# Linear attention in groups of four chunks, with weights laid out as TensorE reads them

## The chip, the cores and the metric

The program runs on one core of one Trainium2 chip. Its metric is device time in microseconds (us), the median of several runs; lower is better. All tensors that matter here are float32.

## The reference

The program is a hybrid network of eight layers over 2048 tokens of 512 features (`x = x + layer(layernorm(x))`): a complex recurrence, a feed-forward layer, a state space scan, the same feed-forward layer, softmax attention, a mixture of experts, a linear attention and the mixture of experts again. Only the seventh, the linear attention, is touched. It has H = 32 heads of D = 64:

```python
qkv = silu(hidden_states @ qkv_w.T).reshape(b, s, H, 3 * D)   # qkv_w: (6144, 512)
q, k, v = split(qkv, 3, axis=-1)                               # then cut into blocks of tokens
def step(state, blk):
    qi, ki, vi = blk
    aw = einsum('bhid,bhjd->bhij', qi, ki) * dd                # scores inside the block, with decay
    intra = einsum('bhij,bhjd->bhid', aw, vi)
    inter = einsum('bhid,bhde->bhie', qi * qd_, state)
    new_state = state * bd_ + einsum('bhsd,bhse->bhde', ki * kd_, vi)
    return new_state, intra + inter
attn = rmsnorm(attn over all 2048 head features, norm_w)
gate = sigmoid(hidden_states @ gate_w.T)                       # gate_w: (2048, 512)
return gate * attn @ out_w.T                                   # out_w: (512, 2048)
```

x has the shape (1, 2048, 512), so that here b = 1 and s = 2048, and the state runs over all 2048 tokens.

## The kernel before

Each layer is a block of its own: every engine has its own program, written out by hand in order, and semaphores are waited on by count. There is a barrier between blocks. The kernel works with its own block length of CH = 128 tokens (a chunk; NCH = 16 chunks), which gives the same values as any other block length. NB = 512 tokens are a quarter (TQ = 4 chunks; TC = 4 quarters). Two heads form a pair: 128 features on the 128 partitions; PAIRS_L = 16 pairs.

The layer has three blocks. `lina` normalizes the residual and transposes it to `lin_z`, features by tokens. `linb` (`linear_heads`) makes the heads. `linc` (`linear_outputs`) multiplies by the output weights.

`linear_heads` holds, for each pair, four kinds of projections (KINDS = 4: query, key, value, gate), each of 128 features by 2048 tokens. A piece (`piece`, L2165) is one kind for one quarter: four matmuls (one for each 128 of the 512 input features) with a 128 x 128 slice of weights `wt` held still and 512 tokens of `z` streaming, into one of two PSUM buffers `pr_ps`; ScalarE takes it out through Silu or Sigmoid (`piece_out`, L2259). The trace shows every float32 matmul as two records and a transpose as one. The weights arrive as rows of features (`wr`), so that before the first piece of a kind TensorE transposes four 128 x 128 blocks (`weight`, L2157, with its records under L2162) and ScalarE copies them to `wt` (`weight_out`, L2255). These five uses of `pr_ps` in each kind make the 20 USES of a pair.

While pair n is scanned, the pieces of pair n + 1 are projected: between the two halves of each chunk stands one piece. `body` (L2227) runs for every chunk c:

- `chunk_first` (L2177): scores of both heads (`s_ps`, L2185, 64 rows each, two heads in the two halves of the array), a transpose of the keys (L2188) and one of the values (L2189) to `tr_ps`. ScalarE brings them out as `kt`, times a decay (two instructions, L2271), and `vt` (L2273). VectorE makes `aw` = scores times decay (L2363).
- the piece of the next pair, and after each fourth the weights of the next kind.
- `chunk_second` (L2191): values times `aw` into `o_ps` (L2201, 64 columns each), the state of the chunks before times `qd` into the same (L2207), then the addition of this chunk to the state, `kv_ps` (L2212). VectorE updates the state, one instruction for each head (L2347).

After each fourth chunk ScalarE copies `o_ps` to `osb` (L2279), POOL adds its squares to `squares` (L2147, L2149), VectorE makes `gated` (L2369) and SyncE stores it. At the start of a pair VectorE makes `qd`, all 2048 tokens in one instruction (L2357), ahead of the first `aw`. Before the first pair, POOL fills tables (L2127 to L2140) for which TensorE and ScalarE wait, ScalarE makes decays (L2287), and the 16 pieces of pair 0 are projected with nothing beside them. In the last pair there is no next one, and so no piece.

`linear_outputs` sums the squares on TensorE (L2420), loads `out_w` in four parts of 1 MB and the first gated features in two of 2 MB, transposes 64 blocks of weights (L2429, L2448), waits for all of them (until 4890.4 in the trace), and then does 16 tiles of 128 tokens, 16 matmuls each (L2438).

Of the kernel before, what the change touches and what calls it, by code (L numbers as in the profile page):

```python
# [21 lines left out]
P = 128  # L22
T = 2048
D = 512
# [1998 lines left out]
def linear_heads(nc, g, name, z, squares):  # L2023
# [3 lines left out]
    with Layer(nc, name) as L:  # L2027
        TQ = NB // CH
        USES = KINDS * (TC + 1)
        wr = L.sb("wr", [P, KINDS, D])  # L2030
        wt = L.sb("wt", [P, KINDS, DT, P])
        proj = [L.sb(f"proj{b}", [P, KINDS, T]) for b in range(2)]
        qd = L.sb("qd", [P, T])
# [10 lines left out]
        aw = L.sb("aw", [P, 2, CH])  # L2044
        kt = L.sb("kt", [P, 2, LD])
        vt = L.sb("vt", [P, P])
        state = L.sb("state", [P, 2, P])
# [4 lines left out]
        s_ps = L.ps("s_ps", [P, 2, 4, CH])  # L2052
        tr_ps = L.ps("tr_ps", [P, 4, P])
        kv_ps = L.ps("kv_ps", [P, 4, P])
        o_ps = L.ps("o_ps", [P, 2, NB])
        names = ("w_taken", "pr_done", "pr_out", "consts", "tables0", "tables", "qd_done", "s_done", "aw_done", "tr_done",
                 "vt_done", "kv_done", "state_done", "o_done", "o_out", "gated_done", "sq_step", "sq_done",
                 "norm_loaded", "osb_used", "state_step", "act_passed")
        S = {n: L.sem(n) for n in names}
        (w_taken, pr_done, pr_out, consts, tables0, tables, qd_done, s_done, aw_done, tr_done, vt_done, kv_done,  # L2060
         state_done, o_done, o_out, gated_done, sq_step, sq_done, norm_loaded, osb_used, state_step, act_passed) = (S[n] for n in names)
        w_loaded = [L.sem(f"w_loaded{k}") for k in range(KINDS)]
        saved = [L.sem(f"saved{b}") for b in range(2)]
        block = L.block()
        qkv_rows = g.dram["L1_attn_b_qkv_w"].rearrange("(h c r) i -> h c r i", c=3, r=LD)
        gate_rows = g.dram["L1_attn_b_gate_w"].rearrange("(n p) i -> n p i", p=P)
# [3 lines left out]
        def over_pairs(eng, body):  # L2070

            with eng.Fori(0, PAIRS_L // 2 - 1) as r:
                body(r * 2, 0, False)
                body(r * 2 + 1, 1, False)
            body(PAIRS_L - 2, 0, False)
            body(PAIRS_L - 1, 1, True)

        @block.sync
        def _(sp):
            def load(kind, n):  # L2080
                if kind < 3:
                    for hh in range(2):
                        sp.dma_start(wr[hh * LD:(hh + 1) * LD, kind:kind + 1, :],
                                     qkv_rows[bass.ds(n * 2 + hh, 1), kind, :, :].rearrange("h r i -> r h i")).then_inc(w_loaded[kind], 16)
                else:
                    sp.dma_start(wr[:, kind:kind + 1, :], gate_rows[bass.ds(n, 1), :, :].rearrange("n p i -> p n i")).then_inc(w_loaded[kind], 32)

            def save(n, b, q):
# [5 lines left out]
            def reload(kind, n):  # L2094

                if kind == 0:
                    sp.wait_ge(pr_done, (n - 1) * USES + 1)
                else:
                    sp.wait_ge(pr_done, (n - 1) * USES + (5 * (kind - 1) + 6))
                sp.sem_inc(w_taken, 1)  # L2100
                load(kind, n)
# [3 lines left out]
            for kind in range(KINDS):  # L2105
                load(kind, 0)
            for kind in range(KINDS):
                reload(kind, 1)


            with sp.Fori(0, PAIRS_L // 2 - 1) as r:
                for b in range(2):
                    n = r * 2 + b
                    for q in range(TC):
                        reload(q, n + 2)
                        save(n, b, q)
            for b in range(2):
                for q in range(TC):
                    save(PAIRS_L - 2 + b, b, q)
            for b in range(2):  # L2120
                sp.wait_ge(saved[b], 16 * (PAIRS_L * TC // 2 + 1))
            sp.wait_ge(norm_loaded, 16)

        @block.gpsimd
        def _(pool):
# [17 lines left out]
            def body(n, b, last):  # L2143
# [12 lines left out]
        def _(pe):  # L2156
            def weight(kind, n, use):  # L2157

                pe.wait_ge(w_loaded[kind], n * 32 + 32)
                pe.wait_ge(pr_out, use[0] * USES + (use[1] + 1))  # L2160
                for k in range(DT):
                    last = nc.tensor.transpose(pr_ps[:, use[1] % 2, k * P:(k + 1) * P], wr[:, kind, k * P:(k + 1) * P], g.ident[:, :])  # L2162
                last.then_inc(pr_done, 1)

            def piece(kind, t, n):  # L2165

                use = 5 * kind + t + 1
                pe.wait_ge(pr_out, n * USES + (5 * kind + 2))
                pe.wait_ge(pr_out, n * USES + (use + 1))
                if t == 0:  # L2170
                    pe.wait_ge(pr_out, n * USES + (5 * kind + 3))
                for k in range(DT):
                    last = nc.tensor.matmul(pr_ps[:, use % 2, :], wt[:, kind, k, :], z[:, k, t * NB:(t + 1) * NB],  # L2173
                                            start=(k == 0), stop=(k == DT - 1))
                last.then_inc(pr_done, 1)

            def chunk_first(n, b, c):  # L2177
                m = n * NCH + c
                cols = slice(c * CH, (c + 1) * CH)
                if c == 0:  # L2180
                    pe.wait_ge(pr_out, n * USES + (USES + 2))
                pe.wait_ge(aw_done, m + 1)
                for hh in range(2):
                    rows = slice(hh * LD, (hh + 1) * LD)
# [342 lines left out]
```

## Time and profile before

| | us |
|---|---|
| median of 3 runs (lowest, highest) | 5951.64 (5946.49, 5953.91) |
| the profiled execution | 5950.2 |
| its span | 5948.2 |
| `linb`, from its first instruction to the barrier behind it | 3374.1 to 4860.3 |
| `linc`, to the last output matmul | 4860.3 to 5110.4 |

The profile is of one execution. The times of rows are counted from the start of the span. PE is TensorE's matmuls, PEld its weight loads, DVE VectorE, ACT ScalarE, POOL GpSimd, SP SyncE. PEclk is the clock that TensorE was granted, as a share of 2.4 GHz; 0.50 is 1.2 GHz. A matmul's duration is longer than the step from one to the next, since they are pipelined: the steps are read from start times.

### The profile page before, as it was taken

How to read it: one execution, taken by the hardware profiler on the slowest of the kernel's cores; microseconds unless marked ns; L12 is line 12 of the kernel's file. 1: busy time of each engine (PE TensorE's matmuls, PEld its weight loads, DVE VectorE, ACT ScalarE, POOL GpSimd, SP SyncE). 2: the span in 40 equal slices, each digit the busy share in tenths (PEclk: the TensorE clock that was granted, in tenths of full speed). 3: DMA queues.
4: the chain of work that ended last, by engine and by line, in shares of the span. 5: the costliest groups of instructions: out<-in, count | busy, mean ns of one | idle time of the engine just before them, and what ended most of it. 6: DMA issues, size and time to landing. Idle time of an engine off the chain costs nothing. (4 is left out here: it accounts for less than half of the span.)

```text
span 5948.2 us, 67863 instructions
## 1 busy us (share of the span) xinstructions
PE 5051.6 (85%) x25328; PEld 2536.2 (43%) x25328; DVE 2334.4 (39%) x3377; ACT 1822.7 (31%) x3499; POOL 1525.2 (26%) x951
## 2 busy tenths in 40 slices
PE   6037897799999999859999499999999979689997
PEld 3013343333333332356555245445445444455654
DVE  1853678357666667441221212222222220331111
ACT  2412554211555457421111133333333320121111
POOL 0011000102776772114545201111111110034444
PEclk9568999899999999969999799999999969789998
DMA  1000000000000000037888300000000012348887
GB/s 44 0 18 12 11 0 0 30 0 1 1 1 1 1 1 1 34 125 204 219 220 225 67 20 25 25 21 25 25 23 23 20 68 71 135 128 224 221 225 161
DMA packets 227748, 395.20 MB, mean 66 GB/s; under 512 B 31712, under 2 KB 119776, under 8 KB 226912
## 3 DMA queue, kind: packets, MB, share of 16 engines
q1 hardware_dynamic: 170144, 249.14, 12.6%
q0 software_dynamic: 57344, 142.64, 11.8%
q8 instruction: 158, 2.59, 0.2%
q14 instruction: 102, 0.84, 0.0%
HBM read 288.88 MB, written 107.02 MB: 67 GB/s over the span
## 5 line engine op out<-in xcount | busy, mean ns | idle before, releaser
L2173 PE MATMUL linb_pr_ps<-lin_z,linb_wt 128*128 128x512 f32 x2048 | 944.5, 606 | 9.0 <-ACT linb_wt L2257 9.0
L1365 ACT ACTIVATE attc_prob<-attc_ps 128x512 f32<-128x512 f32 x1024 | 548.9, 597 | 443.2 <-PE attc_ps L1276 442.4
L1239 POOL TENSOR_TENSOR attc_acc<-attc_acc,attc_prob 128x2048 f32<-128x2048 f32 x120 | 547.9, 4566 | 121.6 <-ACT attc_prob L1365 109.3
L1389 DVE TENSOR_REDUCE attc_peak<-attc_ps 128x2 f32<-128x1024 f32 x384 | 469.6, 1225 | 257.9 <-PE attc_ps L1284 257.9
L2173 PEld LDWEIGHTS linb_pr_ps<-lin_z,linb_wt 128*128 128x128 f32 x2048 | 380.6, 196 | 398.6 <-issue 388.7
L1276 PE MATMUL attc_ps<-att_q,att_k 32*128 32x512 f32 x2048 | 528.7, 616 | 0.0
L2347 DVE SCALAR_TENSOR_TENSOR linb_state<-linb_state,linb_sdec,linb_kv_ps 64x64 f32<-64x64 f32 x448 | 125.3, 280 | 859.0 <-PE linb_kv_ps L2212 851.8
L1284 PE MATMUL attc_ps<-att_k,att_q 32*128 32x512 f32 x1536 | 449.9, 663 | 0.0
L2147 POOL TENSOR_TENSOR linb_sq<-linb_osb 128x512 f32<-128x512 f32 x64 | 67.5, 1055 | 1295.1 <-ACT linb_osb L2279 1295.1
L2262 ACT ACTIVATE linb_proj<-linb_pr_ps 128x512 f32<-128x512 f32 x256 | 152.8, 597 | 625.5 <-PE linb_pr_ps L2173 625.4
L1297 PE MATMUL attc_ps<-attc_prob,att_v 128*32 128x256 f32 (+1 forms) x3472 | 316.5, 437 | 0.3 <-ACT attc_prob L1365 0.3
L886 DVE TENSOR_TENSOR_SCAN ssmb_state<-ssmb_decay,ssmb_bu 128x2048 f32<-128x2048 f32 x64 | 279.7, 4409 | 78.9 <-ACT ssmb_decay L833 78.9
L1864 POOL DMA_INDIRECT residual_rows<-moe2c_ye,moe2w_index x128 | 202.1, 1579 | 313.2 <-issue 279.8
L1864 POOL DMA_INDIRECT residual_rows<-moe1c_ye,moe1w_index x128 | 202.0, 1578 | 311.7 <-issue 279.5
L770 PE MATMUL ssmb_y_ps<-ssmb_state,ssmb_diag 128*128 128x512 f32 x512 | 241.2, 618 | 39.9 <-DVE ssmb_state L886 30.0
L1273 PE MATMUL attc_ps<-att_rows,attc_ones 32*128 32x512 bf16 x1024 | 240.8, 391 | 11.0 <-ACT attc_prob L1365 9.4
L1897 PE MATMUL moe2c_gu_ps<-moe2c_xt,moe2w_wgu 128*128 128x256 f32 x1024 | 249.4, 400 | 0.0
L1897 PE MATMUL moe1c_gu_ps<-moe1c_xt,moe1w_wgu 128*128 128x256 f32 x1024 | 245.6, 396 | 0.0
L215 PE MATMUL lrud_y_ps<-lrud_w,lrud_ht 128*128 128x512 f32 x128 | 56.7, 606 | 216.4 <-DMA lrud_bias<-in_L_attn_a_b_out 216.4
L2271 ACT ACTIVATE linb_kt<-linb_tr_ps,linb_kdec 128x64 f32<-128x64 f32 x512 | 133.0, 309 | 322.2 <-PE linb_tr_ps L2189 298.6
L2438 PE MATMUL linc_y_ps<-linc_wt,linc_gt 128*128 128x512 f32 x512 | 220.0, 592 | 1.0 <-ACT linc_wt L2448 1.0
L1897 PEld LDWEIGHTS moe2c_gu_ps<-moe2c_xt,moe2w_wgu 128*128 128x128 f32 x1024 | 203.0, 203 | 28.5
(516 smaller groups left out, 7766.7 us busy)
## 6 DMA issues: line engine op xcount, KB each, us to landing
moe1w_wgu<-in_L_ffn_gate_up_proj SPq DMA_DIRECT2D x32, 1536.0 KB, 12.4
moe2w_wgu<-in_L_ffn_gate_up_proj SPq DMA_DIRECT2D x32, 1536.0 KB, 12.4
moe1w_wd<-in_L_ffn_down_proj SPq DMA_DIRECT2D x32, 512.0 KB, 13.6
gated_features<-linb_gated SPq DMA_DIRECT2D x64, 256.0 KB, 2.1
linc_gt<-gated_features SPq DMA_DIRECT2D x8, 2048.0 KB, 8.3
moe2w_wd<-in_L_ffn_down_proj SPq DMA_DIRECT2D x32, 512.0 KB, 13.3
linb_wr<-in_L_attn_b_qkv_w SPq DMA_DIRECT2D x96, 128.0 KB, 2.6
residual_rows<-residual SPq DMA_DIRECT2D x2, 4096.0 KB, 12.9
```

The lines of the kernel that those rows point to most:

```text
L770: last = nc.tensor.matmul(y_ps[:, t, :], diag[:, s % DIAGS, :], state[:, s % RING, t * NB:(t + 1) * NB], start=(n == 0), stop=(n == N_STAT ...
L886: V.tensor_tensor_scan(state[:, s % RING, :], decay[:, s % RING, :], bu[:, e % 2, :], 0.0, ALU.mult, ALU.add).then_inc(state_done, 1)
L1239: pool.tensor_tensor(acc[:, n % 2, :, :], before, prob[:, U % NP, :, :], ALU.add).then_inc(pool_done, 2 if at == 1 else 1)
L1273: nc.tensor.matmul(ps[:, banks[-1], :], ones16[own, :], rows[own, cols], start=True, stop=False)
L1276: nc.tensor.matmul(ps[:, bank, :], k[own, f, keys], q[own, f, cols], start=False, stop=True).then_inc(s_done, 1)
L1284: last = nc.tensor.matmul(ps[:, bank + h % 2, :], q[own, f, i * P:(i + 1) * P], k[own, f, b * NB:(b + 1) * NB], start=True, stop=True)
L1297: last = nc.tensor.matmul(o_bank[h * DH:(h + 1) * DH, cols], v[:, i, at:at + DH], prob[:, U % NP, h, cols], start=(i == 0), stop=(i == TT ...
L1365: nc.scalar.activation(prob[:, U % NP, h, :], ps[:, n % 3 if at < 0 else at % 6, :], ACT.Exp).then_inc(exp_done, 1)
L1389: V.tensor_reduce(peak[:, w // TT % 2, i % QH, 2 * hp:2 * hp + 2, b], ps[:, bank:bank + 2, :], axis=AX.X, op=ALU.max).then_inc(mx_used, 1)
L1864: pool.indirect_dma_start(out=g.y_dram, out_offset=bass.IndirectOffsetOnAxis(ap=index[:, n // 2, n % 2:n % 2 + 1], axis=0), in_=ye[:, y % ...
L1897: last = nc.tensor.matmul(gu_ps[:, x, part, :], wgu[:, j % PW, x, k, part * IN:part * IN + P], xt[:, j % 2, x, k, :], start=(k == 0), stop ...
L2173: last = nc.tensor.matmul(pr_ps[:, use % 2, :], wt[:, kind, k, :], z[:, k, t * NB:(t + 1) * NB], start=(k == 0), stop=(k == DT - 1))
```

## The change

Nothing outside the layer changes. The parts:

1. The host lays three weights out (`LAYOUT`): qkv_w and gate_w so that the four 128 x 128 slices of each kind stand as TensorE takes them, out_w transposed. `weight`, `weight_out` and `wr` are gone. Each pair's weights come in two transfers (768 KB and 256 KB) into one of two buffers, two pairs ahead.
2. Values are projected token-major: for kind 2 the slices of `z` (128 tokens) are held still and 128 columns of weights stream, 16 matmuls in a piece in place of 4. ScalarE's Silu writes them straight to `vt[b]`; the transpose and the copy of the values are gone.
3. The scan goes by quarters of four chunks. On TensorE: all scores of the quarter, four key transposes (`keys_first`), one piece, the additions of four chunks (`additions`), three pieces, then all outputs of the quarter (`outputs`). ScalarE brings `kt` out with two instructions for four chunks (`keys_out`), VectorE makes `qd` for 512 tokens and `aw` for four chunks (128 x 1024) in one instruction each, and updates the state four times into 8 slots (`SLOTS`), with a wait between one update and the next.
4. `linear_outputs` loads `wt` directly, in four parts, alternating with four parts of the first features; the first tile waits for each part as it comes to it. The 64 transposes and 16 copies are gone.

```diff
-            def weight(kind, n, use):
-                pe.wait_ge(w_loaded[kind], n * 32 + 32)
...
+            def piece(kind, t, n, r, b):
+                use = TC * kind + t
+                if use == 0:
+                    pe.wait_ge(w_loaded[b], r * 32 + 32)
+                pe.wait_ge(pr_out, n * PIECES + (use + 1))
+                if kind == 2:
+                    for c in range(TQ):
+                        for k in range(DT):
+                            last = nc.tensor.matmul(pr_ps[:, use % 2, c * CH:(c + 1) * CH], z[:, k, (t * TQ + c) * CH:(t * TQ + c + 1) * CH],
+                                                    wt[:, b, kind, k, :], start=(k == 0), stop=(k == DT - 1))
+                else:
+                    for k in range(DT):
+                        last = nc.tensor.matmul(pr_ps[:, use % 2, :], wt[:, b, kind, k, :], z[:, k, t * NB:(t + 1) * NB],
+                                                start=(k == 0), stop=(k == DT - 1))
                 last.then_inc(pr_done, 1)
+            def keys_first(n, b, q):
+                m = n * TC + q
+                if q == 0:
+                    pe.wait_ge(pr_out, n * PIECES + (PIECES + 2))
                 pe.wait_ge(aw_done, m + 1)
+                for r in range(TQ):
+                    cols = slice(q * NB + r * CH, q * NB + (r + 1) * CH)
+                    for hh in range(2):
+                        rows = slice(hh * LD, (hh + 1) * LD)
+                        last = nc.tensor.matmul(s_ps[:, hh, r * CH:(r + 1) * CH], proj[b][rows, 1, cols], proj[b][rows, 0, cols],
+                                                start=True, stop=True)
                 last.then_inc(s_done, 1)
+                pe.wait_ge(kt_done, m + 1)
+                for r in range(TQ):
+                    cols = slice(q * NB + r * CH, q * NB + (r + 1) * CH)
+                    last = nc.tensor.transpose(tr_ps[:, r, :], proj[b][:, 1, cols], g.ident[:, :])
+                last.then_inc(tr_done, 1)
+            def additions(n, b, q):
+                m = n * TC + q
+                pe.wait_ge(kt_done, m + 2)
+                pe.wait_ge(state_done, m + 1)
+                for r in range(TQ - 1 if q == TC - 1 else TQ):
+                    last = nc.tensor.matmul(kv_ps[:, r, :], kt[:, r, :], vt[b][:, q * TQ + r, :], start=True, stop=True)
+                last.then_inc(kv_done, 1)
+            def outputs(n, b, q):
...
+            def body(n, r, b, more):
+                for q in range(TC):
+                    keys_first(n, b, q)
+                    if more:
+                        piece(q, 0, n + 1, r + b, 1 - b)
+                    additions(n, b, q)
+                    if more:
+                        for t in range(1, TC):
+                            piece(q, t, n + 1, r + b, 1 - b)
+                    outputs(n, b, q)
...
 # ScalarE, for each quarter: keys_out, the four piece_out, the table at q == 2, quarter_out
 # VectorE, for each quarter:
+                    V.tensor_tensor(qd[...], proj[b][:, 0, cols], qdec[...]).then_inc(qd_done, 1)
                     dve.wait_ge(s_done, m + 1)
+                    V.tensor_tensor(aw[...], s_ps[...], dd[...]).then_inc(aw_done, 1)
+                    update(n, q)
+                    dve.wait_ge(o_out, m + 3)
...
 # linear_outputs, SyncE
+            for j in range(4):
+                fs = slice(j * WF, (j + 1) * WF)
+                sp.dma_start(gt[:, 0, fs, :], g_rows[:, fs, 0:TOK]).then_inc(first[j], 16)
+                sp.dma_start(wt[:, fs, :], w_rows[:, fs, :]).then_inc(w_loaded[j], 16)
+            sp.dma_start(gt[:, 1, :, :], g_rows[:, :, TOK:2 * TOK]).then_inc(loaded[1], 16)
```

## Rows read from the trace of the kernel before

**Rows 1.** The page: busy time, share of the span and instructions of TensorE

```profile
PE 5051.6 (85%) x25328; PEld 2536.2 (43%) x25328; DVE 2334.4 (39%) x3377; ACT 1822.7 (31%) x3499; POOL 1525.2 (26%) x951
```

**Rows 2.** Windows: stretch, length, busy time and records by engine, clock, DMA share, GB/s

```profile
3633.00:3721.80 88.80, 86.94 (x367) 44.45 (x366) 22.78 (x51) 30.67 (x79) 10.54 (x8) 0.98 0.07 24
4786.20:4856.30 70.10, 49.83 (x221) 31.58 (x220) 21.74 (x51) 13.70 (x53) 12.62 (x8) 0.53 0.04 15
4860.30:4890.40 30.10, 20.14 (x96) 17.40 (x97) 0.23 (x2) 9.53 (x17) 0.00 (x0) 0.57 0.80 279
3728.70:3735.60 6.90, 6.90 (x23) 3.37 (x22) 0.87 (x3) 1.27 (x4) 0.00 (x0) 0.75 0.00 0
2528.00:2567.00 39.00, 39.00 (x182) 37.44 (x181) 8.82 (x27) 8.78 (x15) 0.00 (x0) 0.50 0.44 157
```

**Rows 3.** Timeline, TensorE, two chunks within a pair: start, us from there, line, records

```profile
3756.01 0.44 PE L2201 MATMUL linb_o_ps<-linb_aw,linb_vt 128*64 128x128 f32 x4
3756.38 0.49 PE L2207 MATMUL linb_o_ps<-linb_qd,linb_state 128*128 128x128 f32 x2
...
3757.03 0.49 PE L2185 MATMUL linb_s_ps<-linb_proj 64*128 64x128 f32 x4
3757.45 0.33 PE L2188 MATMUL linb_tr_ps<-ident,linb_proj 128*128 128x128 f32 x1
...
3757.73 3.60 PE L2173 MATMUL linb_pr_ps<-lin_z,linb_wt 128*128 128x512 f32 x8
3761.26 0.44 PE L2201 MATMUL linb_o_ps<-linb_aw,linb_vt 128*64 128x128 f32 x4
...
3766.93 0.44 PE L2201 MATMUL linb_o_ps<-linb_aw,linb_vt 128*64 128x128 f32 x4
```

**Rows 4.** Timeline, all engines, the first chunk of a pair

```profile
3724.61 2.93 DVE L2357 TENSOR_TENSOR linb_qd<-linb_proj,linb_qdec 128x2048 f32<-128x2048 f32 x1 [0.35 <-DVE linb_gated L2369]
...
3727.93 0.44 PE L2201 MATMUL linb_o_ps<-linb_aw,linb_vt 128*64 128x128 f32 x4 [1.86 <-DVE linb_aw L2363]
...
3729.57 5.13 PE L2173 MATMUL linb_pr_ps<-lin_z,linb_wt 128*128 128x512 f32 x8
```

**Rows 5.** Timeline, trains of small matmuls in the mixture of experts

```profile
2625.07 0.53 PEld L1790 LDWEIGHTS moe1b_lane_ps<-moe1b_split,moe1b_lane 128*128 128x128 f32 x4
...
2527.91 3.68 PE L1560 MATMUL moe1a_lg_ps<-moe1a_rwt,moe1a_zt 128*128 128x64 f32 x16
...
2800.69 2.60 PE L1907 MATMUL moe1c_gu_ps<-moe1c_xt,moe1w_wgu 128*64 128x256 f32 x22
```

**Rows 6.** The page: groups of VectorE and ScalarE, with busy us, mean ns

```profile
L1389 DVE TENSOR_REDUCE attc_peak<-attc_ps 128x2 f32<-128x1024 f32 x384 | 469.6, 1225 | 257.9 <-PE attc_ps L1284 257.9
L2347 DVE SCALAR_TENSOR_TENSOR linb_state<-linb_state,linb_sdec,linb_kv_ps 64x64 f32<-64x64 f32 x448 | 125.3, 280 | 859.0 <-PE linb_kv_ps L2212 851.8
L2271 ACT ACTIVATE linb_kt<-linb_tr_ps,linb_kdec 128x64 f32<-128x64 f32 x512 | 133.0, 309 | 322.2 <-PE linb_tr_ps L2189 298.6
```

**Rows 7.** Timeline, TensorE, two chunks of the last pair

```profile
4845.93 0.70 PE L2201 MATMUL linb_o_ps<-linb_aw,linb_vt 128*64 128x128 f32 x4 [0.96 <-ACT linb_vt L2273]
...
4850.09 0.70 PE L2201 MATMUL linb_o_ps<-linb_aw,linb_vt 128*64 128x128 f32 x4 [0.96 <-ACT linb_vt L2273]
```

**Rows 8.** Timeline, TensorE, the projections of pair 0

```profile
3388.40 1.11 PE L2162 MATMUL linb_pr_ps<-ident,linb_wr 128*128 128x128 f32 x4 [15.75 <-POOL linb_slope_own L2140]
3396.01 16.73 PE L2173 MATMUL linb_pr_ps<-lin_z,linb_wt 128*128 128x512 f32 x32 [6.50 <-ACT linb_wt L2257]
3412.57 0.60 PE L2162 MATMUL linb_pr_ps<-ident,linb_wr 128*128 128x128 f32 x4
3413.99 13.97 PE L2173 MATMUL linb_pr_ps<-lin_z,linb_wt 128*128 128x512 f32 x32 [0.82 <-ACT linb_wt L2257]
```

**Rows 9.** Transfers, two of four issued together: KB each, us from issue to landing

```profile
att_v<-in_L_attn_a_Wk SPq DMA_DIRECT2D x1, 1024.0 KB, 7.6
att_v<-in_L_attn_a_Wv SPq DMA_DIRECT2D x1, 1024.0 KB, 9.8
```

More of the change, by code:

```diff
@@ L2177, in chunk_first @@
[L2177 to L2181, printed above, removed]
-                pe.wait_ge(aw_done, m + 1)
-                for hh in range(2):
-                    rows = slice(hh * LD, (hh + 1) * LD)
-                    last = nc.tensor.matmul(s_ps[:, hh, 0, :], proj[b][rows, 1, cols], proj[b][rows, 0, cols], start=True, stop=True)
-                last.then_inc(s_done, 1)
-                pe.wait_ge(vt_done, m + 1)
-                nc.tensor.transpose(tr_ps[:, 0, :], proj[b][:, 1, cols], g.ident[:, :])
-                nc.tensor.transpose(tr_ps[:, 1, :], proj[b][:, 2, cols], g.ident[:, :]).then_inc(tr_done, 1)
@@ new lines, in additions @@
+            def additions(n, b, q):
[6 more added lines that the diff above has]
+            def outputs(n, b, q):
+                m = n * TC + q
+                out = o_ps[:, q % 2, :]
+                pe.wait_ge(o_out, m + 1)
+                pe.wait_ge(aw_done, m + 2)
+                for r in range(TQ):
+                    for hh in range(2):
+                        rows = slice(hh * LD, (hh + 1) * LD)
+                        last = nc.tensor.matmul(out[rows, r * CH:(r + 1) * CH], vt[b][:, q * TQ + r, rows], aw[:, hh, r * CH:(r + 1) * CH],
+                                                start=(r == 0), stop=(q == 0 and r == 0), skip_group_check=True)
+                pe.wait_ge(qd_done, m + 1)
+                pe.wait_ge(state_done, m + 2)
+                for r in range(TQ):
+                    c = q * TQ + r
+                    if c >= 1:
+                        last = nc.tensor.matmul(out[:, r * CH:(r + 1) * CH], state[:, c % SLOTS, :], qd[:, r * CH:(r + 1) * CH],
+                                                start=False, stop=True, skip_group_check=True)
+                last.then_inc(o_done, 1)
@@ L2247, in _ @@
+            over_pairs(pe, body)
         @block.scalar
@@ L2288, in _ @@
             table(0, 0)
-            weight_out(0, (0, 0))
             for kind in range(KINDS):
@@ L2412, in _, with tile @@
             for b in range(2):
-                sp.wait_ge(w_loaded[b], 32)
-                sp.wait_ge(loaded[b], 16 * (T // TOK // 2))
+                sp.wait_ge(loaded[b], 16 * (T // TOK // 2 - 1 + b))
         @block.tensor
         def _(pe):
+            def tile(b, s, used, fresh):
+                pe.wait_ge(y_used, used)
+                for f in range(FT):
+                    if fresh and f % WF == 0:
+                        pe.wait_ge(first[f // WF], 16)
+                        pe.wait_ge(w_loaded[f // WF], 16)
+                    last = nc.tensor.matmul(y_ps[:, s, :], gt[:, b, f, s * P:(s + 1) * P], wt[:, f, :],
+                                            start=(f == 0), stop=(f == FT - 1))
+                last.then_inc(y_done, 1)
             pe.wait_ge(ones_ready, 1)
```

337 lines of the change are left out of this document (122 added, 215 removed).

## The prediction

> **What bounds the kernel now.** I read the page first: TensorE is busy 85% of the span, the others 39% or less [rows 1]. The change touches only the linear attention, so I asked for windows by stretch next. One pair of heads takes 88.8 us, of which TensorE is busy 86.9 at a clock of 0.98; VectorE is busy 22.8, ScalarE 30.7, POOL 10.5 (first row of [rows 2]). Fifteen pairs go like this, one after the other. The last pair, which has no projections beside it, takes 70.1 us at a clock of 0.53: a chain of waits (second row of [rows 2]). Then 30.1 us pass before the first output matmul, with the DMA engines at 0.80 and 279 GB/s (third row of [rows 2]). So three quarters of what follows is a question of TensorE's own time, and I went to its timeline.
>
> A chunk is a period of 5.25 us (3756.01 to 3761.26) with no idle time [rows 3]. By start times: outputs 0.37 (L2201), state and additions together 0.65 (L2207 to L2185), scores 0.42, transposes 0.28, and the piece 3.53. In the piece eight records of 512 columns take 3.60 us, the last one about 0.59, so the step is (3.60 - 0.59) / 7 = 0.43 us for 512 columns, and 0.107 for 128. Now count the small work by that step: outputs and scores are two side-by-side pairs of records each, state, additions and transposes six records, in all ten steps, 1.1 us; the piece is 3.44. That is 4.52 us, and the period is 5.25: 0.73 us are in none of the streams. They lie where the shape in the array changes (128 x 128 to 64-column halves, back, to 64-row halves, to transposes): four changes in a chunk, 0.18 us each. The trace shows nothing else there. Beside it, each fourth chunk takes 5.67 us (3761.26 to 3766.93), 0.42 more, for the weight transposes.
>
> At a pair's start there is one real stall. VectorE makes qd for 2048 tokens (2.93 us) before the first aw; TensorE idles 1.86 us for it, and behind it the clock falls, in the next chunk: eight records last 5.13 us in place of 3.60 [rows 4], at a granted 0.75 (fourth row of [rows 2]). Two long chunks, 3.4 us for a pair: 88.7 = 16 x 5.25 + 4 x 0.42 + 3.4 - 0.4 (the last addition, which is left out, and roundings).
>
> **The change part by part.** *The scan and the pieces.* The same records remain, less four value transposes in a quarter and four weight transposes. A pair after the change, in steps of TensorE:
> - three kinds of pieces, 96 records of 512 columns by 0.43: 41.3;
> - value pieces, 128 records of 128 columns. Now each has a weight load of 128 columns beside only 128 streaming. The nearest row: four loads in 0.53 us, the last 0.19, a step of 0.113 [rows 5] (L1790). At the low clock, 16 records with only 64 columns streaming take 3.68, the last about 0.42, a step of 0.217, in which only the load can be the limit; at the full clock that is 0.109 [rows 5] (L1560). I take 0.112: 14.3 (against 13.8 before);
> - scores 32 and outputs 32 side-by-side pairs by 0.107: 6.8. That such pairs stay side by side in a long train is shown by 22 records of 256 columns in 2.60 us, where one after the other they would need 4.7 [rows 5] (L1907);
> - key transposes 16, additions 30, state 30, by 0.112: 8.5;
> - shape changes, four in a quarter and no longer in a chunk: 16 x 0.18 = 2.9.
>
> Sum 73.8, against 88.7: 14.9 less. 48 shape changes give 8.6 of it, the stall 3.4, the weight transposes 1.7, the value transposes 1.8, and the value pieces take 0.5 back. The first of the fifteen pairs has no stall now, so 15 x 14.9 - 3.4 = 220 us. Ends: if tiled trains load their weights between the steps, a side-by-side pair costs 0.21 and not 0.107, 6.8 a pair or 102 less gain; if shape changes cost nothing when no wait stands beside them, 40 more.
>
> *What hides the rest.* In front of the additions PE waits for kt. Its cover is scores, transposes and one piece: 1.1 + 0.6 + 3.4 = 5 us. On ScalarE are queued ahead of it the copy of the outputs (0.6), then two kt instructions of 256 elements, which I put at 0.45 each (309 ns at 64 elements [rows 6]); with latencies 3.3 us, and 4.8 where the table of the next pair stands ahead. Hidden, by 0.2 us at the least. In front of the outputs PE waits for aw and the state. VectorE has the gating (1.6), qd of 512 (2.93 / 4 = 0.7), aw of 1024 (1.2 by the reduction of the same shape from PSUM [rows 6] (L1389)), four updates of two (0.28 each [rows 6] (L2347), with waits 2.8 in all), 6.3 us; the cover from the additions on is three pieces, 10.3. So qd, which now stalls a pair, is hidden; late next is kt, at no price as long as ScalarE is not 2 us later. Weights come two pairs ahead, 80 us for transfers of 1 MB; SyncE's saves queued behind a reload don't wait, since the pieces that it waits for were done a quarter before.
>
> *The last pair.* Without pieces the quarter is a chain at the low clock (step 0.213, shape change 0.35): scores 2.1, transposes 1.25, kt 1.2, additions 2.1, updates 3.0, state into outputs 2.3: 12 us, 48 for four, less 1 for what is left out at both ends, against 70.1, in which a chunk is 4.16 [rows 7]. 22 us less (by 10 to 28, as kt and the updates are slower or the clock recovers).
>
> *The start.* TensorE has its weights at 3388.4 and needs not wait 6.50 us for ScalarE's first copy: 3396.01 - 3388.40 = 7.6. Each later kind starts 3413.99 - 3412.57 = 1.4 earlier, and one set of transposes goes at the end (0.9) [rows 8]. Less the value pieces' 0.5: 12 us. ScalarE's decays still stand before its first Silu, but two PSUM buffers cover them.
>
> *The output stage.* Before the first tile now stand 1.5 MB and not 8. All four parts are 6 MB: at 279 GB/s (third row of [rows 2]) the last lands at 4860.8 + 22.5 + 2 = 4885; at 1 MB in 2.2 us, the difference of two transfers in flight [rows 9], 12 us earlier. The tile itself is 32 x 0.43 = 13.8 and starts after the sums (7 us), cold. So it ends between 4884 and 4888, where now it ends at 4890.4 + 13.8 = 4904. I take 19 (16 to 21). Fifteen tiles behind it are as before, each fed ahead.
>
> Sum: 220 + 22 + 12 + 19 = 273. From the profiled execution, 5950.2, it gives 5677; that lies 1.4 us under the median, so 5679 as a median.
>
> The Trainium skill speaks against part 2 of the change ("TensorE: Matmul & The Clock Gate", Back-to-back issue gap): for pairs of weight load and matmul at 128 columns it gives about 81 ns, where the matmul alone has 56. By that ratio, 1.45, the value pieces would be an estimated 0.155 us a record. The trace here disagrees with it in the L1790 row, 0.113.
>
> **The rivals.** *A, the loads show.* Behind a load that changes with each record, part of the load is not covered. For it: state and additions, four such records, take 0.65 us, 0.16 each [rows 3]. Against: 0.18 of that 0.65 is a shape change, and L1790. Price: 0.05 x 2048 records = 100 us, 5779. It is what the skill's ratio would do.
>
> *B, the excess belongs to the records, not to the changes of shape*: the 0.73 us in a chunk stay when chunks are grouped. Price 15 x 8.6 = 129 us: 5808. Against: the L1907 and L1790 trains.
>
> *C, the clock falls in the value pieces.* For it: under 39 us of 64-column records and transposes, TensorE busy all along, the granted clock was 0.50 (fifth row of [rows 2]). Against: those stream for half of each step; here the step is full, as in the chunk at 0.98. Price: 64 pieces of 32 x 0.213 = 6.8 in place of 3.6: 205 us, 5884.
>
> *D, slower: a wait for kt in each quarter.* ScalarE does osb, the table, and kt in order, and if their latencies add up to more than the one piece in front of the additions covers, TensorE idles in all 60 quarters and the clock falls after each, as at a pair's start now. One such fall costs 1.7 us behind 1.86 of idling [rows 4]. The gain is 273 / 60 = 4.6 us a quarter, so from a wait of 2.9 us on the kernel is slower; ScalarE's chain would need 8 us and not 3.3 to 4.8. At 3.5 us of waiting, 5.2 x 60 = 312: 5991. For it: the wait is new, and three pieces that could cover it stand behind it.
>
> **How the numbers follow.** The forecast 0.78 (own range 5645 to 5740: better shape changes on one side, half of the tiled loads on the other), A 0.07, B 0.05, C 0.05, D 0.05. The predicted time is 5679. The range 5640 to 5785 takes in the forecast and A, and leaves out B, C and D, with a little of the forecast. What this kernel's times can tell from no change is about 0.2%, 12 us. Faster by more than that are the forecast, A, B and C: 0.94; within it, C or D near its break-even: 0.01; slower 0.05.
>
> **What would show it.** A pair of 74 us, clock near 1.00; 32 records of a value piece within 3.6 us; no idle time of PE before L2201's successor at the pair's start; a last pair of 48 us; the first output tile done 24 to 28 us after the block starts; and VectorE's qd at 0.7 us. PE idle before the additions, with kt as its releaser, would speak for D; a granted clock under 0.8 in the third quarter of each pair for C; a step of 0.15 or more in the value pieces for A; quarters of 20 us and more with no idle time for B. If the moving of the chunks makes a stage after it later (both end with the same barrier, so I see none), the sum is wrong too.

## The result, and the profile after

| | before | after |
|---|---|---|
| median of 4 runs each (lowest, highest), us | 5952.77 (5946.49, 5955.22) | 5676.69 (5664.62, 5686.34) |
| the profiled execution, us | 5950.2 | 5669.14 |
| its span, us | 5948.2 | 5667.4 |

The ratio is 0.9537, 95% interval 0.9513 to 0.956. The forecast was 5679, with a range of 5640 to 5785.

I split both spans at the same points, by start times of TensorE's instructions:

| stretch | before | after | gain | forecast |
|---|---|---|---|---|
| end of `lina`'s transposes to the first scores | 86.8 | 75.3 | 11.5 | 12 |
| first scores of pair 0 to those of pair 15 | 1327.0 | 1123.2 | 203.8 | 220 |
| the last pair, to the start of `linc` | 74.3 | 35.3 | 39.0 | 22 |
| `linc`, to its last output matmul | 249.3 | 229.0 | 20.3 | 19 |
| everything else | | | 6.2 | 0 |
| sum (the difference of the spans) | | | 280.8 | 273 |

The sum is right to 3%, but two of its terms are off by 16 and 17 us in opposite directions. "Everything else" is code that no kernel here touches; in the eleven traces of this document it takes between 4196.9 and 4220.0 us, so that the 6.2 says nothing of the change. TensorE has more records than before and is busy for less time (against [rows 1]); the instruction queue fetched more (158 packets, 2.59 MB before). From the page of the kernel after:

```profile
PE 4820.4 (85%) x26288; PEld 2581.4 (46%) x26288; DVE 2362.7 (42%) x3233; ACT 1644.4 (29%) x2764; POOL 1527.4 (27%) x951
...
q8 instruction: 214, 3.51, 0.3%
```

TensorE's timeline, one quarter in which values are projected. It answers to [rows 3]; L2204 are outputs, L2211 state, L2177 scores, L2183 key transposes, L2159 value pieces, L2192 additions:

```profile
3705.11 1.09 PE L2204 MATMUL linb_o_ps<-linb_aw,linb_vt 128*64 128x128 f32 x16
3706.13 1.16 PE L2211 MATMUL linb_o_ps<-linb_qd,linb_state 128*128 128x128 f32 x8
3707.22 1.16 PE L2177 MATMUL linb_s_ps<-linb_proj 64*128 64x128 f32 x16
3708.31 0.66 PE L2183 MATMUL linb_tr_ps<-ident,linb_proj 128*128 128x128 f32 x4
3708.80 3.74 PE L2159 MATMUL linb_pr_ps<-linb_wt,lin_z 128*128 128x128 f32 x32
3712.38 1.06 PE L2192 MATMUL linb_kv_ps<-linb_vt,linb_kt 128*128 128x128 f32 x8
3713.27 10.88 PE L2159 MATMUL linb_pr_ps<-linb_wt,lin_z 128*128 128x128 f32 x96
3724.08 1.09 PE L2204 MATMUL linb_o_ps<-linb_aw,linb_vt 128*64 128x128 f32 x16
```

No row has an idle time. The first 32 value records take 3712.38 - 3708.80 = 3.58 us, 0.112 each, as I had chosen. The 96 behind them take 10.81, 0.06 more than 96 x 0.112, with the beginning of a shape change at their end. Two rows of the page for VectorE (busy us, mean ns):

```profile
L2331 DVE TENSOR_TENSOR linb_qd<-linb_proj,linb_qdec 128x512 f32<-128x512 f32 x64 | 90.3, 1412 | 90.4 <-ACT linb_proj L2249 75.8 <-DVE linb_gated L2339 12.7
L2334 DVE TENSOR_TENSOR linb_aw<-linb_s_ps,linb_dd 128x1024 f32<-128x1024 f32 x64 | 78.3, 1224 | 2.6 <-PE linb_s_ps L2177 0.5
```

The pairs after are not all alike. By the starts of their first scores they take 73.8, 75.9, 75.4, 76.3, 73.8, 76.2, 73.8, 75.7, 73.8, 76.0, 75.4, 75.7, 73.8, 73.8, 73.8 us. Seven are as forecast and eight are longer by 1.6 to 2.5; this is where the 16 us went. Windows of the first pair (pair 0), of the first 4.8 us of pair 2 and of its rest, then of the last pair and of the first output tile (columns as in [rows 2]):

```profile
3445.40:3519.70 74.30, 74.24 (x436) 48.68 (x438) 22.97 (x41) 19.74 (x34) 7.90 (x6) 1.00 0.07 26
3595.20:3600.00 4.80, 4.80 (x24) 3.32 (x25) 2.35 (x3) 1.85 (x3) 1.32 (x1) 0.64 0.58 198
3600.00:3671.00 71.00, 71.00 (x411) 46.39 (x411) 21.07 (x39) 17.83 (x32) 7.91 (x6) 1.00 0.05 17
4568.60:4599.10 30.50, 19.92 (x206) 16.38 (x204) 20.91 (x42) 5.71 (x13) 12.58 (x8) 1.00 0.09 35
4603.80:4624.70 20.90, 20.66 (x58) 12.88 (x59) 0.48 (x3) 1.46 (x2) 0.00 (x0) 0.70 0.99 343
```

What ends TensorE's idle time is read from its waits. Over the scan, and then the start of pair 2 in the timeline:

```profile
PE linb_s_ps L2177 <- issue: 12.7, 6, 2.4
```

```profile
3595.19 1.66 PE L2177 MATMUL linb_s_ps<-linb_proj 64*128 64x128 f32 x16 [2.08 <-issue]
```

"issue" is time in which the engine waited for nothing that the profile shows: no semaphore and no data. The six places are the starts of pairs 2, 4, ... 12, where TensorE's loop over two pairs (L2073) begins again. Behind two of them, in pairs 2 and 10, the granted clock falls as well, for 1.6 us more each. The trace has the branch itself, on TensorE's sequencer (count, shortest, median and longest ns). In the kernel before (L2240) its median was 208.

```profile
L2073 PEldq COMPARE_BRANCH  x7: 76/3600/3949, 3591.3 to 4493.1; - x7
```

TensorE's loop has 1784 instructions in the trace now and had 1597. One of the page's two instruction queues (q8, 16 KB a packet) goes with this loop: in the six passes behind long jumps (3592 to 4493) it moves 54 packets, nine a pass. In the kernel before it moves none in the six repeated passes (3630 to 4690).

```profile
q8 instruction: 54, 0.88, 0.4%
```

### The profile page after: what moved, and what is told of

Same layout as the page of the kernel before. It is cut to its first block and busy times, and to the rows that moved or that the text cites. A ratio compares the mean times of both kernels' runs of the same rounds, so it can differ in the third digit from the quotient of the medians.

```text
span 5667.4 us, 66951 instructions
## 1 busy us (share of the span) xinstructions
PE 4820.4 (85%) x26288; PEld 2581.4 (46%) x26288; DVE 2362.7 (42%) x3233; ACT 1644.4 (29%) x2764; POOL 1527.4 (27%) x951
## 5 line engine op out<-in xcount | busy, mean ns | idle before, releaser
L2163 PE MATMUL linb_pr_ps<-lin_z,linb_wt 128*128 128x512 f32 x1536 | 677.8, 595 | 16.4 <-POOL linb_slope_own L2133 16.4
L2163 PEld LDWEIGHTS linb_pr_ps<-lin_z,linb_wt 128*128 128x128 f32 x1536 | 286.1, 191 | 342.1 <-issue 324.8
L2339 DVE SCALAR_TENSOR_TENSOR linb_gated<-linb_osb,linb_norm_w,linb_proj 128x512 f32<-128x512 f32 x64 | 94.4, 1474 | 668.1 <-ACT linb_osb L2266 668.1
L2140 POOL TENSOR_TENSOR linb_sq<-linb_osb 128x512 f32<-128x512 f32 x64 | 70.1, 1095 | 1039.0 <-ACT linb_osb L2266 1039.0
L2249 ACT ACTIVATE linb_proj<-linb_pr_ps 128x512 f32<-128x512 f32 x192 | 114.7, 597 | 517.2 <-PE linb_pr_ps L2163 517.2
L2159 PE MATMUL linb_pr_ps<-linb_wt,lin_z 128*128 128x128 f32 x2048 | 233.8, 275 | 0.0
L2159 PEld LDWEIGHTS linb_pr_ps<-linb_wt,lin_z 128*128 128x128 f32 x2048 | 231.2, 192 | 0.5 <-issue 0.5
L1297 PEld LDWEIGHTS attc_ps<-attc_prob,att_v 128*32 128x32 f32 x3472 | 69.0, 109 | 340.2 <-ACT attc_prob L1365 173.0
```

The costliest lines, as they stand in the source:

```text
L1297: last = nc.tensor.matmul(o_bank[h * DH:(h + 1) * DH, cols], v[:, i, at:at + DH], prob[:, U % NP, h, cols], start=(i == 0), stop=(i == TT ...
L2159: last = nc.tensor.matmul(pr_ps[:, use % 2, c * CH:(c + 1) * CH], z[:, k, (t * TQ + c) * CH:(t * TQ + c + 1) * CH], wt[:, b, kind, k, :], ...
L2163: last = nc.tensor.matmul(pr_ps[:, use % 2, :], wt[:, b, kind, k, :], z[:, k, t * NB:(t + 1) * NB], start=(k == 0), stop=(k == DT - 1))
```

## The experiments

Theory: the loop's body has become too long for what TensorE's sequencer keeps, so the jump back waits for instructions to be fetched again. Rivals: the new order, the dense issue of the value pieces, or the weight transfers at a pair's start. Further experiments take the forecast's terms one by one. Unless said otherwise a kernel is derived from the one after. Medians of the kernel before in the two timed groups: 5947.31 and 5949.73.

**The loop written out.**

```diff
-            over_pairs(pe, body)
+            for n in range(PAIRS_L):
+                body(n, n // 2, n % 2, n < PAIRS_L - 1)
```

> The changed kernel with TensorE's loop over pairs written out (16 bodies, no branch back); the other engines keep their loops. In the changed kernel's trace the branch at the end of TensorE's loop body takes 3.3 to 3.9 us (0.2 us in the kernel before), TensorE then idles 1.9 to 2.5 us at six pairs' starts, and twice the clock falls behind it (1.6 us each): 16 us in all. Theory: the body has become too long for what holds TensorE's instructions, so that the jump back has to fetch them, and straight code is fetched ahead. Then every pair takes 73.8 us, no idle time of 2 us at a pair's start, and the time is 16 us less (5653 beside 5669). Rival: the idle time is a wait for another engine that stands at the same place (VectorE's or ScalarE's own loop ends there too): then it stays, and the time stays within 3 us. A third way: straight code is fetched late as well, and small gaps appear all over: slower than the changed kernel.

Measured: 5649.76 (5645.8 to 5655.59), ratio 0.9512 (0.9495 to 0.9528), 0.0025 or 15 us under that of the kernel after (the medians are 27 apart, from different groups of runs, and the two intervals overlap, so that the proof is in the trace). Every one of the fifteen pairs takes 73.8 us; the scan takes 1106.9, which is 16.3 less. The transfers and the order of work are untouched, and the start of a pair has no idle time:

```profile
3587.37 1.16 PE L2211 MATMUL linb_o_ps<-linb_qd,linb_state 128*128 128x128 f32 x8
3588.46 1.16 PE L2177 MATMUL linb_s_ps<-linb_proj 64*128 64x128 f32 x16
```

**A short loop.** Three of four matmuls of the value projection are left out, so that the values are wrong.

```diff
-                        for k in range(DT):
-                            last = nc.tensor.matmul(pr_ps[...], z[:, k, ...], wt[:, b, kind, k, :], start=(k == 0), stop=(k == DT - 1))
+                        last = nc.tensor.matmul(pr_ps[...], z[:, c, ...], wt[:, b, kind, c, :], start=True, stop=True)
```

> The changed kernel with three quarters of the value projections left out (each 128 x 128 block of values is made from 128 of the 512 input features, so the values differ from the reference's): TensorE's loop is kept, but its body is shorter by 384 instructions, shorter than that of the kernel before. It asks whether the length of the body makes the slow branch. Theory of the length: branches of about 0.2 us as in the kernel before, no idle time at pairs' starts, no instruction fetches after the first pass, each pair 73.8 - 10.7 = 63.1 us, so 16 x 10.7 + 16 = 187 us less than the changed kernel. Rival (something else in the new order, the train of small matmuls ahead of the branch): branches of 3.5 us stay, 171 us less, and the six stalls are still there.

Measured: 5496.2 (5491.52 to 5497.79), ratio 0.9251 (0.9235 to 0.9266). That is 180 us less by the medians and 170 by the ratios, where 187 and 171 had been set against each other: the time does not decide. The trace does. The pairs are 63.7 (for 63.1) and all alike, still in a loop, now of 1400 instructions, and q8 moves nothing in its repeated passes:

```profile
L2073 PEldq COMPARE_BRANCH  x7: 76/208/226, 3557.6 to 4322.5; - x7
```

**One in four left out** (`for k in range(3)` in place of `DT`; one run), to move an end of the limit.

> The kernel after, with one in four matmuls of the value projection left out (one of the four input slices of 128 features). TensorE's loop over two pairs then has 1656 instructions in the trace, where the kernel after has 1784 (branches of 3.3 to 3.9 us), the kernel before 1597 and the kernel with three in four left out 1400 (branches of 0.2 us). Theory, the length of the loop decides and the limit lies between 1597 and 1784: the branch either is 0.2 us and all fifteen pairs are alike, or it is 3.3 to 3.9 in six of the pairs; each answer moves one end of the limit to 1656. Work: 32 records of 0.112 less in a pair, 3.6 us, a pair of 70.2, 16 pairs 57 less. With short branches 5677 - 57 - 16 = 5604, with long ones 5620. Rival, the value pieces' dense issue of instructions and not the length makes the branch wait: they are as dense as before, so it stays above 3 us: 5620.

Measured: 5593.61 in one run, nearer to the 5604 of short branches. Its fifteen pairs are 70.2 each, the branches are short, and q8 moves nothing in the repeated passes, with value pieces as dense as in the kernel after. The rival falls, and the limit lies between 1656 and 1784 instructions, for these bodies.

```profile
L2073 PEldq COMPARE_BRANCH  x7: 76/208/213, 3583.6 to 4426.3; - x7
```

**The kernel before, lengthened** (one run): nothing of the change in it, only a longer body.

```diff
-                nc.tensor.transpose(tr_ps[:, 0, :], proj[b][:, 1, cols], g.ident[:, :])
+                for _ in range(4):
+                    nc.tensor.transpose(tr_ps[:, 0, :], proj[b][:, 1, cols], g.ident[:, :])
```

> The kernel before, with each key transpose made four times in place of once, so that TensorE's loop has 192 instructions more: 1789 and not 1597, about as many as after. Nothing else of the change is in it. Work: 48 transposes of 0.11 us more in each of 16 pairs, 5.4 us a pair, 87 in all. Theory, the length of the loop decides: the branches take over 3 us here too (0.2 in the kernel before), and there are 16 KB instruction fetches in every pass. Their price is small here: TensorE waits for the first aw at a pair's start anyway, behind 2.93 us of qd, so that scores that come 2 us later fill part of that wait: 5950 + 87 = 6037, at most 16 more. Rival, the branch is long because of something else in the new loop (its order, its value pieces, the transfers beside it): branches of 0.2 us, 6037.

Measured: 6003.17. Four of its six jumps back take 4.9 to 5.1 us, two 0.2:

```profile
L2241 PEldq COMPARE_BRANCH  x7: 83/4917/5126, 3632.8 to 4747.9; - x7
```

```profile
3638.15 0.49 PE L2185 MATMUL linb_s_ps<-linb_proj 64*128 64x128 f32 x4 [2.08 <-issue]
...
3642.70 0.44 PE L2202 MATMUL linb_o_ps<-linb_aw,linb_vt 128*64 128x128 f32 x4
```

So the length does it, in a kernel that has none of the new order. The fetches go with the jumps: the four passes behind long ones (from 3633, 4185, 4373 and 4560) have nine q8 packets each, 36 in all, and the two behind short ones (3817 to 4185) have none. Why the same body is fetched again in four passes and not in two is not explained.

```profile
q8 instruction: 36, 0.59, 0.3%
```

The jump costs little here, as expected: where scores come 2.08 us late, the wait for the first aw is gone. The size was missed: 50 us more than before and not 87. The transposes were counted about right: a pair without any stall takes 90.3, and 85.3 (before, without its stall) + 48 x 0.107 is 90.4. But of the stall of 3.4 us only 1.6 is left in pairs 3 to 6, whose clock stays at 1.00, where it was 0.98 in every pair before but the first and the last. In pairs 8 to 13 it still falls, to 0.98. The piece behind an idle time of 1.53 us takes 3.60 us here, where it took 5.13 [rows 4]:

```profile
3734.63 0.44 PE L2202 MATMUL linb_o_ps<-linb_aw,linb_vt 128*64 128x128 f32 x4 [1.53 <-DVE linb_aw L2364]
...
3736.44 3.60 PE L2173 MATMUL linb_pr_ps<-lin_z,linb_wt 128*128 128x512 f32 x8
```

The last pair, with 48 transposes more, takes 67.4 us in place of 74.3. Its clock falls to 0.50 as it did before, but is back at 1.00 by 4875, where in the kernel before it stays at 0.50 to the end of the pair. Two windows of it:

```profile
4850.00:4866.00 16.00, 12.56 (x56) 8.70 (x55) 4.25 (x11) 3.02 (x12) 2.12 (x2) 0.50 0.00 0
4875.00:4907.00 32.00, 19.92 (x155) 14.13 (x153) 12.16 (x30) 7.84 (x30) 6.29 (x5) 1.00 0.05 17
```

```profile
4874.29 0.44 PE L2202 MATMUL linb_o_ps<-linb_aw,linb_vt 128*64 128x128 f32 x4 [0.96 <-ACT linb_vt L2274]
...
4877.45 0.44 PE L2202 MATMUL linb_o_ps<-linb_aw,linb_vt 128*64 128x128 f32 x4 [0.96 <-ACT linb_vt L2274]
```

In the second window the idle time is the same 0.96 us as in [rows 7], but a chunk takes 3.16 us at a granted 1.00, not 4.16 at 0.50.

**Are shape changes the price?** Scores and transposes alternate by chunk again, with the same records.

```diff
+                pe.wait_ge(kt_done, m + 1)
                 for r in range(TQ):
                     ...                      # the two scores of chunk r
-                last.then_inc(s_done, 1)
-                pe.wait_ge(kt_done, m + 1)
-                for r in range(TQ):
+                    if r == TQ - 1:
+                        last.then_inc(s_done, 1)
                     last = nc.tensor.transpose(tr_ps[:, r, :], proj[b][:, 1, cols], g.ident[:, :])
```

> The changed kernel with one thing undone: scores and key transposes alternate chunk by chunk (scores of both heads, transpose, four times) in place of all scores and then all transposes. The same instructions, six more changes of shape in each quarter. Theory of the prediction (0.18 us for each change of shape, whatever stands around it): 1.1 us a quarter, 64 quarters, 69 us more. Rival B (the excess belongs to the records): within 5 us of the changed kernel. A cost of only the load that isn't covered (0.107 a change) would give 41 us.

Measured: 5749.03 (5745.79 to 5752.34), ratio 0.9676 (0.966 to 0.9693). By the medians it is 72 us more than the kernel after, for 69 expected. Undisturbed pairs take 78.0, 4.2 more for 24 changes: 0.175 each. Scores and transposes of a quarter take 2.63 us (3723.07 to 3725.70), where after they take 1.58 (3707.22 to 3708.80), and no idle time is shown between them:

```profile
3723.07 0.49 PE L2178 MATMUL linb_s_ps<-linb_proj 64*128 64x128 f32 x4
3723.49 0.33 PE L2182 MATMUL linb_tr_ps<-ident,linb_proj 128*128 128x128 f32 x1
3723.75 0.49 PE L2178 MATMUL linb_s_ps<-linb_proj 64*128 64x128 f32 x4
...
3725.70 0.50 PE L2159 MATMUL linb_pr_ps<-linb_wt,lin_z 128*128 128x128 f32 x3
```

**The piece in front of the additions moved behind them.**

```diff
-                    if more:
-                        piece(q, 0, n + 1, r + b, 1 - b)
                     additions(n, b, q)
                     if more:
-                        for t in range(1, TC):
+                        for t in range(TC):
```

> The changed kernel with the additions right behind the key transposes, and all four pieces behind them: the same instructions, but no piece covers ScalarE's kt. It puts in place the wait of rival D. In the last pair of the changed kernel, where no piece stands there either, TensorE idles 1.04 us at this place. Expected: 1.0 to 1.2 us in each of 60 quarters, 60 to 75 us more, the clock staying at 1.00. Rival: a gap of 1 us in each quarter lets the clock fall, with 1.6 us more at each: 160 us more.

Measured: 5756.83 (5754.36 to 5761.11), ratio 0.9672 (0.9656 to 0.9689), 80 us over the kernel after, where I expected 60 to 75. Undisturbed pairs take 79.1, 5.3 more, of which four waits of 1.04 to 1.11 us are 4.3. The granted clock stays at 1.00 behind these waits, also in the last pair of the kernel after, which has the same wait:

```profile
3513.18 0.94 PE L2192 MATMUL linb_kv_ps<-linb_vt,linb_kt 128*128 128x128 f32 x6 [1.04 <-ACT linb_kt L2255]
```

```profile
3450.80:3529.90 79.10, 74.83 (x430) 48.31 (x430) 22.74 (x41) 19.39 (x33) 7.90 (x6) 1.00 0.06 24
```

Of the other 1.0, about 0.7 is the end of the transposes (0.66 us long, where the next work starts after 0.49), which the wait no longer overlaps, four times 0.17. That share is worked out from the start times; no run separates it.

**The kernel before, with qd by quarters**: the one edit that was to remove the stall at a pair's start.

```diff
-                V.tensor_tensor(qd[:, :]..., q_all, ...).then_inc(qd_done, 1)
                 for c in range(NCH):
+                    if c % TQ == 0:
+                        V.tensor_tensor(qd[:, c * CH:(c + TQ) * CH]..., q_all[:, c:c + TQ, :], ...).then_inc(qd_done, 1)
```

> The kernel before with one part of the change alone: VectorE makes qd for 512 tokens ahead of each quarter, in place of 2048 ahead of the pair. Theory: the 2.93 us of qd are what the first aw of a pair waits for; with a quarter of it (0.9 to 1.5 us) the idle time of 1.86 us and the fall of the clock behind it (1.7 us) go: 14 pairs by 3.2 to 3.4, 45 to 48 us less. Rival: the gating of the last quarter before it (1.6 us, slowed by POOL) already makes aw late; then a rest of the idle time stays, the clock falls as before, and the gain is 15 to 25 us.

Measured: 5924.42 (5909.4 to 5932.27), ratio 0.9945 (0.9925 to 0.9964): 25 us by the medians, 33 by the ratio, and not 45 to 48. In the trace the scan to pair 15 is 29 us shorter and the last pair 3 longer. Pairs take 86.1 and 87.1 to 87.6 in turn, where 85.3 would be free of stalls. The starts of two pairs:

```profile
3729.08 1.63 DVE L2370 SCALAR_TENSOR_TENSOR linb_gated<-linb_osb,linb_norm_w,linb_proj 128x512 f32<-128x512 f32 x1 [4.96 <-ACT linb_osb L2279]
...
3731.06 1.33 DVE L2360 TENSOR_TENSOR linb_qd<-linb_proj,linb_qdec 128x512 f32<-128x512 f32 x1 [0.35 <-DVE linb_gated L2370]
...
3732.78 0.44 PE L2201 MATMUL linb_o_ps<-linb_aw,linb_vt 128*64 128x128 f32 x4 [0.26 <-DVE linb_aw L2364]
...
3817.64 0.31 ACT L2271 ACTIVATE linb_kt<-linb_tr_ps,linb_kdec 128x64 f32<-128x64 f32 x1 [2.48 <-issue]
...
3820.34 0.44 PE L2201 MATMUL linb_o_ps<-linb_aw,linb_vt 128*64 128x128 f32 x4 [1.70 <-ACT linb_vt L2273]
```

At the first, gating and qd together still keep aw back by 0.26 us. At the second, every other pair, ScalarE gets its instructions late ("issue" again, 2.48 us), and vt is what TensorE waits for. The other instruction queue (q14) moves packets of 8 KB at 3815.9 and 3818.0, the first inside that wait and the second inside one of 1.76 us right behind it. It moves five in each repeated pass here and in the kernel before, and none in those of the kernel after, where ScalarE's loop has 136 instructions in place of 290. The profile does not say whose instructions they are. In the kernel before the late instructions were hidden behind the longer qd. The expected gain was half hidden by the next wait.

**The kernel before, with the new `linear_outputs` alone** (and out_w transposed by the host).

> The kernel before with part 4 of the change alone: out_w laid out by the host, loaded in four parts with the first features, no transposes in the output block. Expected 20 us less than the kernel before, by the change's own trace (from the block's start to its last matmul 249.5 before, 229.2 after). Rival: the gain came from something that the new scan leaves behind, such as a warmer TensorE at the block's start; then under 15 us.

Measured: 5925.57 (5921.49 to 5936.39), ratio 0.9953 (0.9936 to 0.9969), 24 us less by the medians and 28 by the ratio, for 20 expected. In the trace `linc` to its last output matmul takes 230.1 for 249.3, 19.2 less, and none of the layer's other stretches moved by over 1 us (the untouched rest of the program took 6.7 more in this execution). It waits 1.23 and 0.27 us for weights, where the kernel after has no such wait.

**The better version.** The loop written out, pair 0's pieces no longer behind POOL's tables, and ScalarE's decays between those pieces.

```diff
-            pe.wait_ge(consts, N_CONSTS)
             for kind in range(KINDS):
                 for t in range(TC):
                     piece(kind, t, 0, 0, 0)
+            pe.wait_ge(consts, N_CONSTS)
...                                          # over_pairs(pe, body) written out; the decays in `scalar` moved
```

> The written-out TensorE program of the run above, and pair 0's projections no longer wait for POOL's tables: TensorE starts them when z and the weights are there, and ScalarE makes its decays between them (half after the queries, half after the keys, the table after the values). TensorE idles 16.4 us ahead of the first piece now; weights land about 4 us into the block, so 8 us of it go. Expected 5645, 8 us less than with the loop alone written out, if two PSUM buffers cover ScalarE's decays (5.9 us against 6.9 of two pieces). Rival: ScalarE's changes of table and decays stall TensorE by as much as is won: no difference to that run.

Measured: 5635.55 (5635.01 to 5649.66), ratio 0.9492 (0.9472 to 0.9512), the best here of the kernels that do all the work. From `lina`'s last transposes to the first scores it takes 65.8 us, where the written-out kernel takes 75.3: 9.5 less, for 8 expected. TensorE now waits for weights:

```profile
3370.91 22.99 PE L2163 MATMUL linb_pr_ps<-lin_z,linb_wt 128*128 128x512 f32 x48 [6.31 <-DMA linb_wt<-in_L_attn_b_gate_w]
```

## Why the prediction came out right, and where it was wrong

- **The undisturbed pair: right.** 73.8 forecast, 73.8 measured in every pair once the loop is written out. Value records 0.112 for 0.112, shape changes 0.175 for 0.18 (measured between scores and transposes, in the alternating kernel), outputs and scores as trains of side-by-side pairs: outputs start 1.02 us before the state does, eight steps of 0.107 and one change.
- **"15 x 14.9 - 3.4 = 220": wrong by 16.** The step that failed is the sum's silence on the loop: I counted every instruction's time on the array and none for the jump back over a longer body. It is six times 1.8 to 2.4 us of idling (12.7), plus a clock that falls behind two of them (0.64 in the window above), 1.6 us each. The kernel written out, the two with shorter bodies and the lengthened one pin it to the length.
- **"The quarter is a chain at the low clock ... 12 us": mis-sized.** The chain was right and the clock was not: a quarter takes 7.8 us at a granted 1.00, four 31 and not 48. The term was 39, not 22; my upper bound, 28, was too low as well. With TensorE's parts halved and the rest left, my own terms give 2.1 + 1.25 + 2.1 + 2.3 = 7.75, half of it 3.9, and 4.2: 8.1 us a quarter (an estimate), against 7.8 measured, so that little but the clock was wrong. The subtraction also slipped by one: 70.1 less 47 is 23. I took the clock of [rows 7] over to a chain with other gaps. Three of its rows in the kernel after (DVEq is VectorE's sequencer, which reports the updated state):

```profile
4578.92 1.16 PE L2192 MATMUL linb_kv_ps<-linb_vt,linb_kt 128*128 128x128 f32 x8 [1.04 <-ACT linb_kt L2257]
4580.47 1.09 PE L2204 MATMUL linb_o_ps<-linb_aw,linb_vt 128*64 128x128 f32 x16 [0.39 <-DVE linb_aw L2334]
4582.90 1.13 PE L2211 MATMUL linb_o_ps<-linb_qd,linb_state 128*128 128x128 f32 x8 [1.34 <-DVEq L2323]
```

- **"2.93 / 4 = 0.7" for qd: wrong, without a price.** It takes 1.41 us in the mean and 0.69 at its shortest. Three pieces cover VectorE's 7 us, so that it costs nothing here; in the kernel before with qd by quarters it takes 1.33 at the start shown, ahead of an aw that comes 0.26 us late.
- **The stall at a pair's start** is gone. But that qd alone made it was too simple: gating stands in the same queue, and ScalarE's late instructions hid behind both.
- **The start and the output stage: right** (11.5 for 12, 20.3 for 19). The first tile's addition starts 4627.74, 23.9 us after the block, for 24 to 28 forecast, at 343 GB/s and not 279. (With 1 MB in 2.2 us the parts land 9 us earlier, not the 12 I wrote; the term does not use it.)
- **A** falls by 0.112 a record, **B** by 73.8 and by 0.175 for a change, **C** by a clock of 1.00 in all pairs but the two behind a slow jump (0.98). **D** falls: over the whole layer TensorE waits 4.1 us for kt (row below), all of it in the last pair, and with the cover taken away the wait is 1.04 us, the clock stays at 1.00, and the price is 80 us, well short of the 273 that D needed.

```profile
L2192 PE MATMUL linb_kv_ps<-linb_vt,linb_kt 128*128 128x128 f32 x480 | 64.4, 276 | 4.1 <-ACT linb_kt L2257 4.1
```

The total came nearer than its terms deserve: a loss of 16 not seen and a gain of 17 not seen cancel. That is luck.

## What to carry to other kernels

Count the changes of tile shape on TensorE as well as its records, 0.18 us each, and group work of one shape as far as the buffers allow. When an edit lengthens the body of a loop, count the body's instructions, and look at the branch's duration, at idle time that ends with "issue" and at the instruction queue's packets in the repeated passes; writing the loop out gave back 16 us of the scan here (the ratio to before fell from 0.9537 to 0.9512). A clock read in one chain of waits isn't the clock of the chain that replaces it: work it out at both levels.

## What the hardware showed that was not expected

- The jump back of TensorE's loop takes 0.2 us with 1400, 1597 and 1656 instructions in the body, and 3.3 to 5.1 with 1784 and 1789 (but for two jumps), and only behind the long jumps is the body fetched again. The Trainium skill ("Runtime: NRT & Kernel Launch", Instruction fetch mechanics) says that a taken branch to a target outside the current window of two pages must wait for a fetch of the target page. The runs agree on the wait and not on the sizes: with pages of 256 instructions, as it has them, two would let none of these bodies pass, and the 2048 instructions that it gives for TensorE would let all of them pass.
- With redundant transposes in it, a chain of waits got its clock back: in the later part of the last pair, 4.16 us a chunk became 3.16, at a granted 0.50 and 1.00 with the same idle time of 0.96. This is from one run of one kernel.
- VectorE's qd of 512 tokens takes 0.69 us at its shortest and 1.52 in the median. Of the 64 the shortest is the only one that no POOL instruction overlaps. Each of the other 63 starts while a POOL instruction runs and ends 0.54 to 0.56 us behind the end of that instruction, whether they overlap by 0.38 us or by 0.98: as if its work began only then. No run changes POOL's work alone, so that the cause is read from the trace and not tested. The shortest and one of the long ones (3730.89 against the addition's end at 3730.34):

```profile
3445.45 0.69 DVE L2331 TENSOR_TENSOR linb_qd<-linb_proj,linb_qdec 128x512 f32<-128x512 f32 x1 [75.82 <-ACT linb_proj L2249]
...
3728.75 1.59 POOL L2142 TENSOR_TENSOR lin_squares<-lin_squares,linb_sq 128x512 f32<-128x512 f32 x1
3729.37 1.52 DVE L2331 TENSOR_TENSOR linb_qd<-linb_proj,linb_qdec 128x512 f32<-128x512 f32 x1 [0.15 <-DVE linb_gated L2339]
```
